# A routed expert layer behind cross-attention: routing weights sent with the scattered rows, gathers that add into the residual, b2 as a product

## What is computed

```python
def _L0_ffn_ref(x, Wg, bg, W1, b1, W2, b2):
    xf = x.reshape(-1, D)
    probs = jax.nn.softmax(xf @ Wg + bg, axis=-1)
    w, idx = jax.lax.top_k(probs, TOP_K)                 # TOP_K = 2
    w = w / jnp.sum(w, axis=-1, keepdims=True)
    comb = jnp.sum(jax.nn.one_hot(idx, E, dtype=xf.dtype) * w[..., None], axis=1)
    h = jax.nn.relu(jnp.einsum('nd,edh->enh', xf, W1) + b1[:, None, :])
    y = jnp.einsum('enh,ehd->end', h, W2) + b2[:, None, :]
    out = jnp.einsum('end,ne->nd', y, comb)

x = x + jnp.tanh(g_xattn[0]) * xattn(_layernorm(x), ctx_1024, ctx_1024, mask, Wq, Wk, Wv, Wo, 16)
x = x + jnp.tanh(g_ffn[0]) * _L0_ffn_ref(_layernorm(x), Wg, bg, W1, b1, W2, b2)
```

## Time and profile before

| | |
|---|---|
| median of 3 runs | 1154.45 us |
| the profiled execution | 1155.27 us |
| its span in the profile | 1153.5 us |
| granted clock of PE, mean | 0.921 |
| DVE, PE, ACT, POOL busy | 81%, 76%, 68%, 62% of the span |
| steps 0 to 127 (row_max of the first to that of the last batch) | 45.1 to 958 us |
| first `hidL` of chunk 3 | 1015.84 us |
| last gather issued | 1146.05 us |

### The profile page before, as it was taken

One profiled execution on the slowest core, in us unless ns is written; L12 is line 12 of the kernel. 1 busy time (PEld: TensorE's weight loads), 2 busy tenths in 40 slices (PEclk: granted clock), 3 DMA queues, 4 the chain that ended last, 5 costly groups with the idle time before them and its releaser, 6 DMA issues.

```text
span 1153.5 us, 33826 instructions
## 1 busy us (share of the span) xinstructions
PE 881.5 (76%) x11840; PEld 674.7 (58%) x11840; DVE 939.9 (81%) x2160; ACT 785.6 (68%) x1627; POOL 710.6 (62%) x701
## 2 busy tenths in 40 slices
PE   6787888798788888877897887878898767555560
PEld 4465665566566766666675656666676556444440
DVE  3888898898989897978888989978798987646633
ACT  3877778777677878786887667766887564444540
POOL 3143455547365666564658787755758787778775
PEclk9998899999999999999999998999998897778975
DMA  8367756555467765453445455554445465477773
GB/s 173 75 172 196 206 146 171 153 159 157 130 172 197 207 179 158 107 131 96 116 116 147 121 161 131 128 129 103 109 122 160 119 172 154 145 202 211 209 205 103
DMA packets 250791, 174.53 MB, mean 151 GB/s; under 512 B 39168, under 2 KB 232192, under 8 KB 250624
## 3 DMA queue, kind: packets, MB, share of 16 engines
q1 hardware_dynamic: 242432, 155.57, 50.9%
q0 software_dynamic: 8192, 16.79, 4.9%
HBM read 75.42 MB, written 63.84 MB: 121 GB/s over the span
## 4 chain that ended last, share of the span: by engine, by line
DVE 24%; issue 13%; PE 13%; POOL 8%; ACT 8%; SPq 3%; DMA 2%; DVEq 0%; POOLq 0%; ACTq 0%
PE bank L90 4%; POOL arena L1033 4%; PE bank L92 3%; PE bank L91 3%; DVE qL L726 3%; POOL hidL L1072 2%; DVE vL L901 2%; DVE row_max L929 2%; DVE otL L955 2%; DVE arena L909 2%; DVE x_back L949 2%; POOL slots L1020 2%; DVE row_sum L917 1%; SPq L1153 1%; ACT qH L545 1%
## 5 line engine op out<-in xcount | busy, mean ns | idle before, releaser
L1078 POOL TENSOR_TENSOR ptL<-pt,ptH 128x512 f16<-128x512 f32 x128 | 148.8, 1162 | 250.9 <-ACT pt L651 250.6
L726 DVE TENSOR_TENSOR qL<-bank,qH 128x512 f16<-128x512 f32 x256 | 173.7, 681 | 51.7 <-ACT qH L545 49.5
L545 ACT ACTIVATE qH<-bank 128x512 f16<-128x512 f32 x256 | 152.9, 599 | 43.8 <-PE bank L92 42.6
L1084 POOL TENSOR_TENSOR prob<-prob,row_inv 128x512 f32<-128x512 f32 x128 | 134.9, 1054 | 52.4 <-DVE row_inv L935 52.3
L1020 POOL DMA_INDIRECT slots<-x2hat,slot x128 | 128.1, 1001 | 31.9 <-issue 29.9
L90 PE MATMUL bank<-ptH,vdH 128*128 128x64 f16 x1024 | 120.4, 202 | 33.6 <-DVE arena L909 23.6
L1033 POOL DMA_INDIRECT arena<-slots,slot x128 | 123.1, 962 | 36.1 <-issue 29.7
L90 PE MATMUL bank<-arena,hidH 128*128 128x128 f16 x396 | 83.6, 240 | 69.6 <-POOL hidL L1072 66.9
L90 PEld LDWEIGHTS bank<-ptH,vdH 128*128 128x128 f16 x1024 | 107.9, 118 | 41.2 <-DVE arena L909 27.6
L1072 POOL TENSOR_TENSOR hidL<-arena,hidH 128x512 f16<-128x512 f32 x99 | 115.7, 1169 | 12.2 <-ACT hidH L595 10.8
L91 PE MATMUL bank<-ptL,vdH 128*128 128x64 f16 x1024 | 120.4, 202 | 0.0
(11 more groups left out here) (158 smaller groups left out, 3399.5 us busy)
## 6 DMA issues: line engine op xcount, KB each, us to landing
arena<-expert_weights SPq DMA_DIRECT2D x99, 321.0 KB, 3.1
slots<-zeros SPq DMA_DIRECT2D x60, 512.0 KB, 3.4
vdH<-vH SPq DMA_DIRECT2D x256, 64.0 KB
vdL<-vL SPq DMA_DIRECT2D x256, 64.0 KB
arena<-slots SPq DMA_DIRECT2D x99, 128.0 KB
slots<-arena SPq DMA_DIRECT2D x99, 128.0 KB
x_raw<-in_x SPq DMA_DIRECT2D x16, 256.0 KB, 4.1
ctx_raw<-in_ctx SPq DMA_DIRECT2D x16, 256.0 KB, 4.6
```

The costliest lines, as they stand in the source:

```text
L545: act.activation(qH[:, g % 2, 2 * j + g2, :, h2, :], bk("Q", g, h)[:, :].rearrange("p (b q) -> p b q", b=GB), ACT.Copy).then_inc(s_q_high, 1)
L726: dve.tensor_tensor(qL[at], bk("Q", g, h)[:, :].rearrange("p (b q) -> p b q", b=GB), qH[at], ALU.subtract).then_inc(s_q_low[h % 2], 1)
L1078: pool.tensor_tensor(ptL[:, b % 2, :], pt[:, b % 2, :], ptH[:, b % 2, :], ALU.subtract).then_inc(s_pt_low, 1)
L1084: pool.tensor_tensor(p, p, row_inv[:, b % NPB, :].unsqueeze(2).to_broadcast([P, JG, S]), ALU.mult).then_inc(s_normal, 1)
```

## The change

**Weights travel.** A row of the table grows from 128 to 132 numbers (`ROW`), and so does `x2hat`. DVE copies `pick_weight` of pick 0 into column 128 of `x2hat` (`pick_into_rows`, in the step with i = 1), POOL scatters pick 0 in the steps with i = 3 and 4, DVE copies the weights of pick 1 in the step with i = 5, after the scatters of pick 0 have landed, and POOL scatters pick 1 in those with i = 6 and 7. A unit's rows come back with their weight beside them.

**Scaling.** `y_rows` is written by two DVE instructions a unit (128x128 each, PSUM by a per-row scalar) in place of one of 128x256, and without b2. b2 is split into two fp16 halves once, at steps 3 to 6, is kept in the first two partitions of each expert's weights (the others hold zeros), and enters `y` as one more matmul with `ones16` in front of each half of `expert_out`.

**Gathers accumulate.** `got` and the two DVE instructions of each idx go. POOL's gathers write with `compute_op=ALU.add` straight into `x2_back`. The gather of pick 1 waits for the landing of that of pick 0 and is issued one step later. The store of a group waits for the gathers.

**Rings and loads.** The row ring grows from 3 to 6 buffers; rows and weights of a unit count on one semaphore, so that `turn_slots` waits for both.

**Steps.** All units move one step later (steps 50 to 80, 82 to 112, 114 to 136, 138 to 156, 157 to 167). Where both fall after step 128, two idx share a step: the combining steps are 85 to 100, then 117 to 127 singly and 128, 128, 129, 129, 130, then 141 to 148 in pairs, 161 to 166 in pairs, and 172 and 173 in pairs. The diff, cut to its core:

```diff
-    ready = [GB * (e + 2) + 1 for e in ENDS]
+    ready = [GB * (e + 2) + 2 for e in ENDS]
...
         at = UNIT_STEP[LAST_UNIT[CHUNK_OF[idx // GT]]] + 5
-        steps.append(max(at, steps[-1] + 1) if steps else at)
+        if steps:
+            alone = steps[-1] < B or len(steps) > 1 and steps[-2] == steps[-1]
+            at = max(at, steps[-1] + 1 if alone else steps[-1])
+        steps.append(at)
...
                 for t in range(2):
+                    pe.matmul(bk("y", n)[:, t * D:(t + 1) * D], ones16[:, :], w2[:, 2 * B2_AT:2 * B2_AT + D],
+                              start=True, stop=False, skip_group_check=True)
...
+            def pick_into_rows(g, pick):
+                if pick == 0:
+                    dve.wait_ge(s_weight, g + 1)
+                    dve.wait_ge(s_ln[1]["rows"], g + 1)
+                else:
+                    dve.wait_ge(*picked_scattered(g, 0))
+                dve.tensor_copy(x2hat[:, g % 2, :, D:D + 1], pick_weight[:, g, pick, :].unsqueeze(2)).then_inc(s_pick_in, 1)
...
-                    dve.scalar_tensor_tensor(y_rows[:, n % 2], bk("y", n)[:, 0:2 * D].rearrange("p (t d) -> p t d", t=2),
-                                             1.0 / WS, w_ring[:, n % NW, B2_AT:B2_AT + D].unsqueeze(1).to_broadcast([P, 2, D]), ALU.mult,
-                                             ALU.add).then_inc(s_y_out, 1)
+                    for t in range(2):
+                        last = dve.tensor_scalar(y_rows[:, n % 2, t, :], bk("y", n)[:, t * D:(t + 1) * D],
+                                                 slot_rows[:, n % NW, t, D:D + 1], 1.0 / WS, ALU.mult, ALU.mult)
+                    last.then_inc(s_y_out, 1)
...
-                    dve.scalar_tensor_tensor(acc, got[:, idx % NG, 0, :], pick_weight[:, cg, 0, ct:ct + 1], acc, ALU.mult,
-                                             ALU.add).then_inc(s_first, 1)
...
-                    dve.scalar_tensor_tensor(acc, got[:, idx % NG, 1, :], pick_weight[:, cg, 1, ct:ct + 1], acc, ALU.mult,
-                                             ALU.add).then_inc(s_both, 1)
...
-                if pick == 0:
-                    if idx >= NG:
-                        pool.wait_ge(s_both, idx - NG + 1)
-                    if g == ENDS[k] - CHUNKS[k] and t == 0:
+                if pick == 0 and t == 0:
+                    if g == ENDS[k] - CHUNKS[k]:
                         pool.wait_ge(*unit_stored(LAST_UNIT[k] - 1))
                         pool.wait_ge(*unit_stored(LAST_UNIT[k]))
-                pool.indirect_dma_start(got[:, idx % NG, pick, :], None, slots[SLOTS_IN[k]],
-                                        bass.IndirectOffsetOnAxis(ap=slot[:, g, pick, t:t + 1], axis=0)
-                                        ).then_inc(s_gather[idx % NG], 16)
+                    pool.wait_ge(s_x2_back[g % 2], 16 * (g // 2 + 1))
+                if pick == 1:
+                    pool.wait_ge(*gathered(idx, 0))
+                pool.indirect_dma_start(x2_back[:, g % 2, t, :], None, slots[SLOTS_IN[k]],
+                                        bass.IndirectOffsetOnAxis(ap=slot[:, g, pick, t:t + 1], axis=0),
+                                        compute_op=ALU.add).then_inc(s_gather[idx % GT], 16)
...
-                if 3 <= i < 3 + GT and within(g - 2, GROUPS):
-                    scatter(g - 2, i - 3, 0)
-                    scatter(g - 2, i - 3, 1)
-                if combine_at(s) is not None:
-                    gather(combine_at(s), 0)
-                    gather(combine_at(s), 1)
+                if i in (3, 4, 6, 7) and within(g - 2, GROUPS):
+                    pick, t = (0, 2 * (i - 3)) if i < 5 else (1, 2 * (i - 6))
+                    scatter(g - 2, t, pick)
+                    scatter(g - 2, t + 1, pick)
+                for idx in combines_at(s - 1):
+                    gather(idx, 1)
+                for idx in combines_at(s):
+                    gather(idx, 0)
```

132 lines of the change are left out of this document (74 added, 58 removed).

## The result

The changed kernel takes **1257.53 us** (median of 4 runs, 1255.23 to 1258.9), the kernel before beside it 1153.68: a ratio of **1.0898, 95% interval 1.0878 to 1.0917**, so 104 us slower. The direction was as forecast (1170.5), the size was not: it lies far above the range of 1153 to 1203. The profiled execution took 1255.23 us, its span is 1253.5.

The account below looks back on a forecast made before the run. DVE was taken to bound the attention part and POOL the tail, SP just behind. Terms -14 + 5 + 1 + 24 = +16 on 1155.3 gave 1171.3, or 1170.5 us on the median's level; range 1153 to 1203.

Parts of the forecast that it names:

- DVE's additions go: Removing `x_back` from DVE gives -14 us in the attention part (bounds 0 and 36) and -0.8 at the end.
- two y_rows instructions: On DVE in the attention part: 0.13 us more for each of 69 units, 9 us, a third on the path.
- copies and scatter order: Weight copies of 14 attention-part groups take DVE 6 us, a third on the path; the second copy finds its scatters landed.
- b2 as a product: Two more PE matmuls a unit and the splitting of b2 at step 4 cost +1 us, bounds 0 and 3.
- units a step later: In the tail, chunk 3's first unit comes one step later and waits for its weights too: +2.5 us.
- new order of the tail, with the waits for the last units' stores: POOL stands idle 30.8 us in the tail against 8.7 before, which is +22 us.
- I take 0.96: An accumulating gather's issue on POOL costs 0.96 us, as a plain one does; dearest indirect DMA in the trace 1.215.
- Rival 2: Accumulating gathers are dearer, by 0.26 us of issue (+17) and slower landing (+30); half of both gives 1194.5 us; chance 0.28.
- DVE's new work: Two `y_rows` instructions and the weight copies in the attention part: 15 us, a third on the path, +5, bounds 0 and 15.
- The scatters pass no other DMA on POOL: The moved scatters keep their place among POOL's DMAs; no cost was counted for their order.
- DVE's release: Taking `x_back` off DVE in the attention part gains 14 us, bounds 0 and 36.
- the twelve lone `hidL`: Steps 150 to 161 have no gathers and run at SP's pace, 3.46 us each, leaving POOL 22.7 us idle.

Follow-up runs that it names:

- e4: Kernel before without DVE's two instructions adding gathered rows to the residual, a one-column memset in their place; 0.9895 of the kernel before.
- e12: Changed kernel with one y_rows instruction a unit, both halves scaled by the first half's weight; 1252.0 us, 1.0846 of the kernel before.
- e13: Changed kernel without the weight copies and with the scatters in the old order; 1244.0 us, 1.0773 of the kernel before.
- e9: Changed kernel with plain gathers, one y_rows instruction, no weight copies, old scatter order and no product of b2; 1.0232 of the kernel before.
- e1: Kernel before with every unit and its combining one step later; 1.0038 of the kernel before.
- e15: Changed kernel with plain gathers, one idx a step, both gathers in it, the second into its own buffer; 1.0232 of the kernel before.
- e7: Changed kernel with the residual of groups 8, 12 and 15 fetched five steps ahead instead of one; 1.0840 of the kernel before.
- e14: Changed kernel with plain gathers, so nothing is added to the residual; 1194.0 us, 1.0333 of the kernel before.
- e16: Kernel before with gathers that add into the ring `got`, DVE's additions kept; 1.0437 of the kernel before.
- e17: Changed kernel with plain gathers, one idx a step, one y_rows instruction, no weight copies, old scatter order; 1.0055 of the kernel before.
- e11: Changed kernel run again unaltered, as anchor for three kernels on the same chip; 1258.2 us, 1.0885 of the kernel before.

## Why the prediction was wrong

Its steps, with what was measured (us of the kernel before at 1153 to 1155):

| term | forecast | measured | by |
|---|---|---|---|
| DVE's additions go | -14, -0.8 at the end | -12 | e4 |
| two y_rows instructions | +3 | +6 | e12 |
| copies and scatter order | +2 | +14 | e13 |
| b2 as a product | +1 | nothing | e9 |
| units a step later | in +2.5 | +4 | e1 |
| new order of the tail, with the waits for the last units' stores | +22 | +12 to +20, 29 in the tail | e15 |
| wait for the fetched residual | nothing | +6 to +8 | e7 |
| the gathers' add, its issue time above all | 0 | +64, +51 in e16 | e14, e16 |

With 64 for the add, the measured terms sum to 94 to 104, the result is 103 to 104. They were taken in different surroundings, some of them between chips, so that they come this near is in part luck; and the 14 us that e17 leaves open are more than the fetch's 6 to 8.

**The step that failed** is the sentence "I take 0.96". The prediction bounded the accumulating gather's issue by the dearest indirect DMA of the trace, 1.215 us, which was an outlier of a plain one and no bound at all for an operation that the trace did not show. At 1.556 the 64 gathers of its tail alone make 64 x 0.6 = 38 us, and the others 26 us more. Rival 2 named the right mechanism at 0.28 but with 0.26 us of issue and up to 30 us of landing; pick 1 waited 0.8 us in all for a landing (median 3.6 us), and it was nearly all issue. Of the rival's two halves the dear one was thought cheap and the cheap one dear.

The sentence from the Trainium skill (Collectives: The Full Stack, The bandwidth ceiling), that an add needs two source reads, explains the bandwidth of collectives; read as a rule for this gather, it would have put the cost into the landing. Measured, the landing went from a median of 3.2 us (32 gathers of e14) to 3.6, not towards the double; the packets of the queue went from 8192 to 22528 with the same bytes, the page's list of queues of e14 and of the changed kernel:

```profile
q0 software_dynamic: 8192, 17.06, 5.4%
```

```profile
q0 software_dynamic: 22528, 17.06, 8.3%
```

With 256 indirect DMAs in either, half of them gathers, a gather went from 32 packets to 144, if the scatters kept their 32 (e16, whose scatters are those of the kernel before, shows 22528 too). More to write for POOL is a reading that fits 0.6 us; no run varied the packets, so it is not shown.

**Mis-sized: DVE's new work**, +5 for 20. Of the y_rows part the size was off: one such instruction takes 0.475 us and two 0.684, 0.27 above the one of before, the upper end where the middle was taken, and somewhat more than a third of it is on the path. The copies' own time (0.17 us each) was right, but the step looked only at DVE's instructions and at whether the scatters had landed. "The scatters pass no other DMA on POOL" was not so: pick 1's scatters moved behind the gathers of i = 3 to 5, a chunk's table is complete later, and in the tail they lengthen a step with four gathers. That gives 6 of the 16 us by which the traces of e11 and e13 differ; for the rest no cause is shown.

**DVE's busy time,** 38.6 us down where some 90 were forecast. The additions, 103.3 us, are gone, `y_rows` brought 18.5 and the copies 5.6: that alone would be 79. Most of the other 40 are in four small groups of instructions that took longer each, from 39.2 to 73.1 us together; their means, before and after, in ns: `above` 714 and 1280, `rstd` 245 and 536, `shift` 424 and 687, `picked` 401 and 836. No run shows why, nor that the time depends on it.

**Missed: the fetch.** The prediction's wait at the first gather of a chunk was for the last unit's store, 2.3 and 5.6 us. The gather now writes into the fetched residual, so it must wait for that fetch as well, which SP issues one step before and behind the store of two groups earlier: 5.45 and 8.14 us in those two places and 4.18 at the tail's begin. The wait for the store was sized well: e7, with the fetch out of the way, shows 5.75 us of it at chunk 4 where 5.6 were forecast, and 0.79 at chunk 3 where 2.3 were.

**Right:** DVE's release; the plain step of four gathers (e14's `hidL` at 1063.44 and 1069.49, 6.05 us, forecast 6.1); the twelve lone `hidL` at SP's 3.44 us with 22.8 us of POOL idle (22.7); no wait for pick 0's landing in steps 142 to 149 of the changed kernel. With gathers as quick as it assumed that last point doesn't hold: in e14 pick 1 waited 13 times, 6.9 us in all, where 0.2 were forecast, as landings took up to 5.5 us and not 2.9. With plain gathers the sum would have been off by 22 us, not by 87. DVE's release was right in part by luck: its bound for 840 to 970 us took POOL's 7.7 us of waits from rows that begin at 899 us, while one wait alone, that of `ptL` for ACT, was 16.3 us in the whole stretch.

## What to carry to other kernels

An operation that the trace does not show is not bounded by its dearest relative in the trace; where it stands on the engine that binds and occurs a hundred times, its unknown issue time is the forecast, and one small run that prices it is worth more than the rest of the sum. For a moved DMA, ask when its last one now lands, what waits for that, and which other DMAs now share its step. An instruction that has become slower is a cause only if the stretch around it has become longer too, and a run without it has lost the time. A DMA that writes where an engine used to add inherits all the waits of the target, and on an engine that has no slack.

## What the runs showed of the hardware

- An indirect gather of 128 rows of 512 bytes took POOL 0.957 us, with an add 1.556 us (1541 to 1642 ns in the changed kernel and in e16), whether it added into the residual or into the ring. It landed 3.6 us after its issue (median, 3.2 to 6.4) against 3.2 (2.5 to 5.5, the 32 gathers of e14 for which the trace shows it).
- POOL's `hidL` behind such a gather is shown with 1.76 us in place of 1.17; it begins 0.6 us before the gather's end, so it seems to wait for it and costs nothing beyond.
- A DVE instruction with two SBUF inputs waited behind three POOL instructions in a row, 3.34 us in place of 0.51; the median did not show it, only the mean of the group. The group of batches around it was no longer for it (69.5 us against 69.2).
- Scaling 128x256 from PSUM by a value per row took 0.475 us, two of 128x128 took 0.684.
